# 64-wide attention: the output projection of a batch in two halves in two steps, the next batch's first rounds one step later

## The reference, cut to what matters

```python
def _L1_xattn_ref(input_Q, input_K, input_V, Wq, bq, Wk, bk, Wv, bv, Wo):
    B, S, D, H, DK = (4, 512, 256, 16, 64)
    def _proj(x, W, b):
        y = jnp.einsum('bsd,ed->bse', x, W) + b
        return y.reshape(x.shape[0], x.shape[1], H, DK).transpose(0, 2, 1, 3)
    Q = _proj(input_Q, Wq, bq); K = _proj(input_K, Wk, bk); V = _proj(input_V, Wv, bv)
    scores = jnp.einsum('bhqd,bhkd->bhqk', Q, K) / np.sqrt(DK)
    attn = jax.nn.softmax(scores, axis=-1)
    context = jnp.einsum('bhqk,bhkd->bhqd', attn, V)
    context = context.transpose(0, 2, 1, 3).reshape(input_Q.shape[0], -1, H * DK)
    return jnp.einsum('bse,de->bsd', context, Wo)

x = x + _L1_xattn_ref(_layernorm(x), ctx_1024, ctx_1024, ...)
```

## Time and profile before

| | us |
|---|---|
| median of 3 runs | 1623.09 (1622.76 to 1624.24) |
| the profiled execution | 1632.88 |
| its span, first to last instruction | 1631.1 |
| busy: PE / DVE / ACT / POOL | 1412.1 / 1077.5 / 843.7 / 479.0 |
| weight loads on PE | 1137.2 |
| scores of the 64-wide attention, L403, busy | 70.7 |
| output projection, L440, 384 matmuls | 110.8 busy, 13.85 a batch |
| granted clock, mean | 0.923 |

### The profile page before, as it was taken

How to read it: one execution, slowest core, us unless ns; L and a number is a source line. 1 busy time by engine, 2 the same in 40 slices (tenths; PEclk the granted TensorE clock), 3 DMA queues, 4 the chain that set the end, 5 groups by cost and what they waited for, 6 DMA issues and landing times. The chain is left out here.

```text
span 1631.1 us, 29265 instructions
## 1 busy us (share of the span) xinstructions
PE 1412.1 (87%) x9650; PEld 1137.2 (70%) x9650; DVE 1077.5 (66%) x2480; ACT 843.7 (52%) x1967; POOL 479.0 (29%) x426
## 2 busy tenths in 40 slices
PE   4898883999999969999999996599957899888885
PEld 4666542888888858888888884499945697555553
DVE  4677644666666657777787777644457865588776
ACT  2566542444444537766676765155534453555451
POOL 2111002477777630000000001255422421143343
PEclk8899966999999989999999999699979899899887
DMA  5322116455655456544654444022173010221110
GB/s 148 125 88 83 57 51 221 116 133 138 165 141 133 97 137 160 125 116 116 142 118 111 106 143 137 29 76 78 62 233 124 10 40 27 79 85 61 59 47 26
DMA packets 140110, 168.92 MB, mean 104 GB/s; under 512 B 20136, under 2 KB 131880, under 8 KB 137448
## 3 DMA queue, kind: packets, MB, share of 16 engines
q1 hardware_dynamic: 115032, 131.43, 27.9%
q0 software_dynamic: 16032, 27.01, 7.8%
q10 hardware_dynamic: 8944, 9.17, 1.8%
HBM read 75.66 MB, written 24.12 MB: 61 GB/s over the span
## 5 line engine op out<-in xcount | busy, mean ns | idle before, releaser
L1278 ACT ACTIVATE a_probT<-a_t 128x512 f32<-128x512 f32 x256 | 151.5, 601 | 168.1 <-PE a_t L998 137.8
L1079 DVE TENSOR_REDUCE a_nmax<-a_s 128x2 f32<-128x512 f32 x256 | 170.8, 685 | 98.3 <-PE a_s L994 97.7
L622 ACT ACTIVATE a_prob<-a2f_bank,a_nmax 128x256 f32<-128x256 f32 x256 | 120.1, 479 | 34.1 <-DVE a_nmax L515 34.0
L515 DVE TENSOR_REDUCE a_nmax<-a2f_bank 128x2 f32<-128x512 f32 x128 | 87.9, 687 | 72.0 <-PE a2f_bank L404 72.0
L63 POOL TENSOR_TENSOR a_rstd<-a_veps,minus_half 128x2 f32<-128x2 f32 x24 | 17.2, 715 | 401.2 <-DVE a_veps L57 401.1
L1566 PE MATMUL a2f_bank<-f_rowsT_hi,area_odd_parts 128*128 128x512 f32 x384 | 133.5, 399 | 1.5 <-DVE f_rowsT_lo L1688 1.5
L1863 POOL DMA_INDIRECT x_rows<-early_hn,scatter_row x60 | 129.9, 2166 | 16.4 <-issue 16.4
L1796 ACT ACTIVATE f_gate<-a2f_bank 128x512 f32<-128x512 f32 x64 | 38.3, 599 | 127.2 <-PE a2f_bank L1566 99.1
L1700 DVE TENSOR_TENSOR f_y<-f_gate,a2f_bank 128x512 f32<-128x512 f32 x64 | 44.0, 688 | 79.5 <-ACT f_gate L1796 40.7
L631 ACT COPY a_probT<-a2f_bank 128x512 f32<-128x512 f32 x128 | 76.1, 595 | 20.6 <-PE a2f_bank L412 19.5
L522 DVE TENSOR_SCALAR a_prob<-a_prob,a_rinv 128x256 f32<-128x256 f32 x256 | 83.3, 368 | 4.6
(11 more groups left out here) (432 smaller groups left out, 4507.1 us busy)
## 6 DMA issues: line engine op xcount, KB each, us to landing
area_odd<-in_L_experts SPq DMA_DIRECT2D x15, 1536.0 KB
a_k_hi<-a_k_fresh_hi SPq DMA_DIRECT2D x128, 128.0 KB, 2.4
area_odd_parts<-area_even_parts SPq DMA_DIRECT2D x192, 64.0 KB, 2.6
a_k_lo<-a_k_fresh_lo SPq DMA_DIRECT2D x64, 128.0 KB, 2.4
a_q<-a_q_fresh_lo SPq DMA_DIRECT2D x64, 128.0 KB, 2.4
a_q<-a_q_fresh_hi SPq DMA_DIRECT2D x62, 128.0 KB, 2.4
a_ctxT<-in_ctxT SPq DMA_DIRECT2D x32, 128.0 KB, 2.8
a_ka<-a_k_hi SPq DMA_DIRECT2D x64, 64.0 KB, 2.6
```

Of the source, the lines that this page charges most:

```text
L515: nc.vector.tensor_reduce(nmax[:, u % NPROB, :], ps_score[u % NB][:, :, :], AX.X, ALU.max, negate=True).then_inc(sem["nmax"], 1)
L622: last = nc.scalar.activation(prob[:, u % NPROB, i, :], ps_score[u % NB][:, i, :], ACT.Exp, bias=nmax[:, u % NPROB, i:i + 1], accum_out=rs ...
L1079: nc.vector.tensor_reduce(nmax[:, u % 2, :, i * PPU + j], ps_s[i][:, :, :], AX.X, ALU.max, negate=True).then_inc(sem["nmax"], 1)
L1278: nc.scalar.activation(probT[:, t % NPT, i, :, :], ps_t[i][:, :, :], ACT.Exp).then_inc(sem["exp"], 1)
```

## The change

- `STEP`: `hT` goes from step 6 to 7, k0 from 7 to 8, q0 from 8 to 9. The other rounds stay. The readers (ACT, DVE) and SP's placing of k0 and q0 move with them.
- `output(b - 1)` is made in two halves, query tile 0 in step 5 and query tile 1 in step 6, 24 matmuls each. The waits stand ahead of the first half, the semaphore `out` is raised by the second.
- ACT's `keep_output(b, 0)` goes from step 5 to step 6, with a new wait for `out`, since the second half still reads `oT_hi`. It stands behind the exponentials of step 6 and ahead of `context_high`.
- DVE's `low_output(b, 0)` and `add(b - 1)` go from step 6 to step 7. `context_low` stays in step 6, and so comes ahead of them.

```diff
-    STEP = {"hT": 6, ("k", 0): 7, ("q", 0): 8, ("k", 1): 10, ...
+    STEP = {"hT": 7, ("k", 0): 8, ("q", 0): 9, ("k", 1): 10, ...
@@ PE
-            def output(b):
-                pe.wait_ge(sem["oT_lo"], (b + 1) * NCH)
...
-                after(pe, sem["xadd"], b)
-                for qt in range(TB):
+            def output(b, qts=range(TB)):
+                if qts[0] == 0:
+                    pe.wait_ge(sem["oT_lo"], (b + 1) * NCH)
...
+                    after(pe, sem["xadd"], b)
+                for qt in qts:
...
-                last.then_inc(sem["out"], 1)
+                if qts[-1] == TB - 1:
+                    last.then_inc(sem["out"], 1)
...
-                    if s == OUT_STEP and not first(b):
-                        output(b - 1)
+                    if OUT_STEP <= s < OUT_STEP + TB and not first(b):
+                        output(b - 1, range(s - OUT_STEP, s - OUT_STEP + 1))
@@ DVE
-                    if s > LAG + 1 and (s - 1 - LAG) % TB == 0:
+                    if s == OUT_STEP + TB:
+                        low_output(b, 0)
+                    elif s > LAG + TB + 1 and (s - 1 - LAG) % TB == 0:
                         low_output(b, (s - 1 - LAG) // TB - 1)
...
-                    if s == OUT_STEP + 1 and not first(b):
+                    if s == OUT_STEP + TB and not first(b):
                         add(b - 1)
@@ ACT
-                    if s > LAG and (s - LAG) % TB == 0:
+                    if s == OUT_STEP + 1:
+                        if not first(b):
+                            act.wait_ge(sem["out"], b)
+                        keep_output(b, 0)
+                    elif s > LAG + TB and (s - LAG) % TB == 0:
                         keep_output(b, (s - LAG) // TB - 1)
```

More of the change, by code:

```diff
@@ L188, in head_attention @@
     NV = TB * E // BANK
-    STEP = {"hT": 6, ("k", 0): 7, ("q", 0): 8, ("k", 1): 10, ("q", 1): 11, ("v", 0): 12, ("k", 2): 13, ("v", 1): 14, ("q", 2): 15,
+    STEP = {"hT": 7, ("k", 0): 8, ("q", 0): 9, ("k", 1): 10, ("q", 1): 11, ("v", 0): 12, ("k", 2): 13, ("v", 1): 14, ("q", 2): 15,
             ("k", 3): NU + 1, ("q", 3): NU + 2, ("v", 2): NU + LAG, ("v", 3): NU + LAG + 1}
@@ L427, in weighted_values @@
                 last.then_inc(sem["pv"], 1)
-            def output(b):
-                pe.wait_ge(sem["oT_lo"], (b + 1) * NCH)
[L431 to L434, removed]
-                after(pe, sem["xadd"], b)
-                for qt in range(TB):
+            def output(b, qts=range(TB)):
+                if qts[0] == 0:
+                    pe.wait_ge(sem["oT_lo"], (b + 1) * NCH)
+                    if first(b):
+                        pe.wait_ge(sem["Wo_lo"], 1)
+                    held = rounds[OUT::NPB][-1]
+                    pe.wait_ge(*consumed(b + 1 if not isinstance(b, int) or b < B - 1 else b, held))
+                    after(pe, sem["xadd"], b)
+                for qt in qts:
                     for c in range(NCH):
```

## The result

| | before | after |
|---|---|---|
| median of 19 runs each | 1624.57 us (1618.57 to 1634.64) | 1632.68 us (1625.05 to 1641.86) |
| ratio, 95% interval | | 1.0041 [1.0024, 1.0058] |
| first scores to the last output projection of the attention | 389.08 us | 394.23 us |
| a steady batch | 49.01 us | 49.57 us |

The change makes the kernel slower by 0.41%, some 6.7 us (3.9 to 9.4). The forecast was +2.7 us and the range ended at 1629.2, so the sign of the sum was right and its size was not; the time, 1632.68 us, lies outside the range.

The account below looks back on a forecast made before the run. PE was taken as the bound. Steady batches +3.0, batch 0 +0.4 and batch 7 -0.7 summed to +2.7 us on a 1623.09 us median: forecast 1625.8 us (+0.17%, chance 0.51), range 1619.4 to 1629.2.

Parts of the forecast that it names:

- The bound: 64-wide attention, batch by batch: PE is the bound, so any PE wait lengthens the run one for one.
- Part 3: Steady batches, k0 on PE: waits 1.0 us for DVE's add instead of 0.47; +0.5 us a batch, +3.0 over six.
- Parts 1 and 2: Steady batches: splitting the projection costs +0.1 us or nothing; scores and transposes ahead of k0 make PE ready 0.83 us later.
- Part 4: Steady batches behind k0: its reads and copies shift later, v0 on PE keeps a 0.7 us margin, cost 0.
- Part 5: Batch 0: k0's placing 2.3 us later, landing taken as 2.46 us, v0 later: +0.4 us (bounds 0 and +2.3).
- Part 6: Batch 7: only the split acts; the 0.68 us wait of scores(9) on ACT goes: -0.7 us (bounds 0 and -1.0).
- The case in which gains and wait cancel: Rival, chance 0.15: chain to k0 0.4 us shorter, k0 waits as long as before; about -0.5 us, 1622.6.
- The cover: Rival, chance 0.19: k0 does not wait for the add, each steady batch gains 0.4; -3.5 us, 1619.6.
- The placing of k0: Rival, chance 0.12: k0's copies land late, v0 waits 1.2 us more in six batches, 2 in batch 0; +11.8, 1634.9.
- The clock: Rival, chance 0.03: the new 1.0 us PE wait lowers the clock, 3 us a batch; +18 us, 1644.

Follow-up runs that it names:

- the repeat: The changed kernel run again with nothing edited, against the kernel before: ratio 1.0045 [1.0018, 1.0072].
- both edits: Changed kernel with ACT's context high part ahead of the output's wait and batch 0's hT, k0, q0 in old steps: 0.9973, again 0.9976, against the kernel before.

## Why the prediction was right, and where it was wrong

**The bound** (PE's waits count one for one): right, and nothing of a wait was absorbed. The rule of the Trainium skill ("Perfetto Trace Analysis", section "Identifying the Most-Contended Engine") was weighed against it: by weight-load busy time PE is at 40.94 of 49.61 us, and a new wait might be swallowed. None was, in any run: 0, 0.47, 0.85 and 2.52 us of idle time at k0 gave batches of 48.47, 49.01, 49.57 and 51.01 us.

**Part 3**, the chain from the second half to k0, was right link by link. Shifted by the 5.75 us between the two projections' starts, `keep_output` was forecast at 762.80 and came at 762.86, `ctx_lo` at 763.84 and came at 763.87, the add at 766.17 and came at 766.20, k0 at 766.90 and came at 767.02. **Parts 1 and 2** held as well: PE would have been ready for k0 at 765.93 (765.57 + 0.36), where 765.90 was forecast, so the split cost nothing that can be seen. The delay of k0 was 1.09 us for a forecast of 1.0; the profile shows 0.85 of it as idle. The old delay, which the prediction took at the 0.47 that the profile shows, was 0.54 by starts. That makes +0.56 us a batch, for a forecast of +0.5.

**Part 4** forecast ACT's wait for the copies at 1.3 to 2 us and a margin of 0.7 us at v0. ACT waited 1.67 to 1.72 us in five batches, and DVE's low part ended 0.68 us ahead of v0. But "cost 0" failed in the first of the six batches: there v0 waited 0.35 and, in the repeat, 0.81 us, which made its interval 0.6 to 1.1 us longer than the others.

**Part 5** is the step that failed most. It forecast +0.4 us for batch 0; +1.74 was measured, and 1.4 to 1.6 by the run with the old steps, at a like clock. The shift of the copies, 2.3 us forecast, was 2.38 (first issue 29.60 and 31.98 us behind the first scores), and the landing taken there, 2.46 us, was measured at 2.47 (625.28 to 627.75). What was wrong was the reading of the 4.4 us of the earlier trace rows. I had put it down to a full queue, which would ease. It was tied to a moment of batch 0 and came again: two issues ahead of the last took 2.51 us and not 1.25, so 1.26 us were lost there, on a chain that the shift had robbed of its slack. The bound of +2.3 for this term held.

**Part 6**: +0.03 us in the last interval, which has one steady wait of +0.56 in it, leaves -0.53 for batch 7, against -0.7. The wait of scores(9) fell from 0.68 to 0.28 us and did not go altogether; only in the run with the add in step 6 did it go.

**The sum.** 3.4 + 1.74 + 0.6 - 0.53 = +5.2 us in the stage, for a forecast of +2.7. That the time, 1632.68 us, is 6.9 above 1625.8 has three parts. The stage lost 2.5 us more than forecast. The kernel before itself had a median of 1624.57 in these runs and not 1623.09, 1.5 us. The last 2.9 us are what the two medians differ by (8.1) beyond the stage (5.2); the ratio makes the loss 6.7, and its interval, 3.9 to 9.4, holds the 5.2. Up to 1.0 us of this can be the clock of batch 0, which favoured the changed kernel in the two profiles. Whether the rest is real stays open; no stage outside this attention was changed, and no run was made on it. **The range** ended at 1629.2 since it had been put around a median of three runs and left the late copies outside, at 0.12: their price in the steady batches didn't come due, but the part of it for batch 0 did. Its ends were also summed a little wrong: the bounds of parts 3, 5 and 6 make 1623.9 to 1629.6, which doesn't reach 1632.68 either. The case in which gains and wait cancel adds up to -0.3 us and not -0.5.

**The rivals.** The cover did not hold by itself; it took one more moved item (the context on ACT, or the add on DVE) to make it hold. The placing of k0 was late only in batches 0 and 1, but the margin in the steady batches was 0.68 us, as the prediction had said, and in the run with the shift alone, where ACT is 1.6 us later, it was used up. The clock stayed at 1.00 in the steady batches of every run.

## What to carry to other kernels

When work is cut up so that another engine need not wait for it, look at what stands behind the new wait in that engine's queue: here a context copy and an add that had nothing to do with the cut were queued behind it, and moving either by a few lines was worth more than the cut. Idle time of 5.6 us on engines off the bound is a place to put such work, and no loss to be removed. A slack measured in steady batches did not hold in batch 0 and in the first pass of the loop. And a wait is best read as a distance between starts: the idle time that the profile shows was up to 0.24 us short of the delay.

## What was not expected of the hardware

**Copies within the chip almost stop shortly behind a packet of the instruction queue.** In the window 621 to 628 of the changed kernel (40 slices of 0.175 us) the transfer rate falls from about 190 to 6 to 29 GB/s for 1.2 us, and the queues show one packet of another kind:

```profile
GB/s 0 0 0 0 0 6 176 193 187 193 217 199 187 187 310 176 164 223 228 176 152 29 6 12 6 12 18 29 187 193 193 176 228 187 187 193 258 187 193 217
...
q1 hardware_dynamic: 1032, 0.94, 60.1%
q8 instruction: 1, 0.02, 1.2%
```

The steady window 770 to 776 has no such packet and no such dip:

```profile
GB/s 0 0 0 0 0 0 0 0 0 0 0 0 0 177 191 177 191 185 232 184 184 184 212 212 184 191 226 246 184 212 171 219 184 198 198 205 212 177 184 205
...
q1 hardware_dynamic: 872, 0.80, 58.3%
```

The packet is recorded 1 to 1.7 us ahead of the dip, in this window and in four others. From 605 to 705 us there are five such packets (0.02 MB) in the profile of before and five in that of after; from 705 to 930, in the later passes of the loop over batches, none in either (one of 0.01 MB, on another instruction queue, comes there); then, in batch 7, which is written out, three in each. So they come in the stretches whose code runs for the first time. In every one of the twelve profiles one stands 33.5 to 35.5 us behind the first scores, whatever the edit. What came with each depends on what was under way: in before, a landing 4.4 us long (630.82 to 635.19) and 0.18 us of wait at v0, though the rate was low for only 0.5 us there; after, in batch 0, the issue that took 1.26 us longer, and 1.96 us of wait at v0; in batch 1, a landing of k0 of 3.63 us (674.25 to 677.88, 2.44 in batch 3) and 0.35 us of wait. In the run with the context in the idle time the landing of k0 was long as well, 3.79 us (622.25 to 626.04), but v0 waited only 0.16. That the packet is the cause is argued from this coincidence in time. No run takes a packet away.

**The clock in batch 0 and at the end of batch 7.** The kernel with both edits was profiled twice. With the same instructions it had 8.5 us at the lower level in batch 0 once and 10.7 once, and a clock of 0.98 in the last interval once and 1.00 once, 79.87 and 78.58 us. In the changed kernel with the old steps in batch 0 the clock from 980 to 990 us was 0.54, nearly all at the lower of the two levels, 1.2 GHz; in the changed kernel it was 1.00 there. No run tells what decides it.
